# A four-layer graph network on one core: one layer's bias moves into centred weights, another's type bias moves from TensorE to VectorE

## The reference

```python
# layer 0: attention over the incoming edges, plus bias
x = layernorm(x + attention(x, edges) + bias)
# layer 1: W1 is 256x256, W2 is 256x128
h_neigh = segment_sum(h[src], dst) / maximum(deg, 1)
x = layernorm(h + relu((concatenate([h, h_neigh]) @ W1 + b1) @ W2 + b2))
# layer 2: one weight matrix for each of 8 edge types
x = layernorm(h + segment_sum((h @ weight[rel])[src], dst))
# layer 3: 3 edge types, 3 node types
parts = [relu(h)] + [segment_sum(where(type == t, relu(h[src] @ W_e[t].T + b_e[t]), 0), dst) for t in range(3)]
agg = concatenate(parts)                          # 512 features
updated = agg @ W_n[node_type].T + b_n[node_type]
x = layernorm(updated + h)
```

## Time and profile before

| | |
|---|---|
| median of 3 runs | 1756.77 us (1755.32 to 1764.27) |
| the profiled execution's own time, its span | 1757.07 us, 1755.0 us |
| PE busy, share of the span | 1439.8 us, 82% |
| PEld | 920.1 us, 52% |
| DVE | 1389.7 us, 79% |
| ACT | 1078.8 us, 61% |
| POOL | 1230.9 us, 70% |
| mean granted TensorE clock | 0.926 |

### The profile page before, as it was taken

How to read it: one execution, slowest core, us unless ns; L and a number is a source line. 1 busy time by engine, 2 the same in 40 slices (tenths; PEclk the granted TensorE clock), 3 DMA queues, 4 the chain that set the end, 5 groups by cost and what they waited for, 6 DMA issues and landing times.

```text
span 1755.0 us, 22874 instructions
## 1 busy us (share of the span) xinstructions
PE 1439.8 (82%) x6228; PEld 920.1 (52%) x6228; DVE 1389.7 (79%) x2964; ACT 1078.8 (61%) x2688; POOL 1230.9 (70%) x910
## 2 busy tenths in 40 slices
PE   2678777877887738888878589999996799999995
PEld 1445544554554526666666445565563455555553
DVE  3889999999999937989788579999997466666663
ACT  0467777777777755999889836666665233333331
POOL 7477666667766737888885188888882678888864
PEclk8799999999999968999888899999999899999998
DMA  5343444444444334777665445555542433333320
GB/s 149 73 93 99 111 107 101 103 106 105 101 110 110 76 105 121 200 193 200 173 192 150 141 105 144 135 151 142 133 122 77 102 90 91 92 95 94 91 72 22
DMA packets 165794, 205.06 MB, mean 117 GB/s; under 512 B 66824, under 2 KB 97919, under 8 KB 165667
## 3 DMA queue, kind: packets, MB, share of 16 engines
q1 hardware_dynamic: 108066, 179.45, 38.3%
q0 software_dynamic: 57600, 24.15, 7.9%
HBM read 147.12 MB, written 70.80 MB: 124 GB/s over the span
## 4 chain that ended last, share of the span: by engine, by line
PE 45%; DVE 24%; issue 11%; ACT 11%; POOL 4%; DMA 3%; SPq 1%; POOLq 0%; DVEq 0%; ACTq 0%
PE po L1211 22%; PE pt L1196 4%; DVE masked L867 4%; PE po L1206 4%; DVE bst L663 4%; PE pb L1434 4%; ACT res L952 3%; DVE run L738 2%; PE po L1269 2%; ACT x L952 2%; POOL slot_all L475 2%; DVE po L707 2%; DVE po L706 1%; DVE y L698 1%; DVE y L703 1%
## 5 line engine op out<-in xcount | busy, mean ns | idle before, releaser
L475 POOL DMA_INDIRECT xs<-target_rows,slot_all x276 | 387.6, 1404 | 192.9 <-DMA xs<-source_rows 112.1
L952 ACT ACTIVATE x<-y,nmr,rst 125x128 f32<-125x128 f32 x800 | 322.6, 482 | 41.6 <-DVE nmr L688 40.2
L1211 PE MATMUL po<-wnt,rt 128*125 128x384 f32 x800 | 305.0, 529 | 0.5 <-ACT rt L989 0.5
L475 POOL DMA_INDIRECT xs<-in_x,src_all x100 | 142.3, 1423 | 121.9 <-issue 121.9
L1211 PEld LDWEIGHTS po<-wnt,rt 128*125 128x125 f32 x800 | 168.2, 210 | 112.5 <-issue 33.4
L1211 PE MATMUL po<-wnt,run 128*125 128x384 f32 x600 | 201.5, 486 | 0.0
L1206 PE MATMUL po<-ball,ones_bf 128*125 128x512 bf16 (+1 forms) x512 | 147.6, 416 | 63.9 <-DVE sel L709 56.1
L1196 PE MATMUL pt<-ident,x 125*128 125x125 f32 x800 | 127.5, 284 | 77.8 <-issue 54.6
L482 POOL DMA_INDIRECT out_rows<-do,last_all x100 | 140.0, 1400 | 72.1 <-issue 52.3
L952 ACT ACTIVATE do<-yd,nmr,rst 125x128 f32<-125x128 f32 x400 | 163.7, 482 | 5.8 <-DVE nmr L688 5.8
L952 ACT ACTIVATE res<-sel,nmr,rst 125x128 f32<-125x128 f32 x400 | 163.6, 482 | 1.7 <-DVE nmr L688 1.7
(11 more groups left out here) (185 smaller groups left out, 3009.8 us busy)
## 6 DMA issues: line engine op xcount, KB each, us to landing
xin<-in_x SPq DMA_DIRECT2D x100, 224.0 KB
out_rows<-res SPq DMA_DIRECT2D x100, 224.0 KB
same<-same_d SPq DMA_DIRECT2D x75, 250.0 KB
source_rows<-so SPq DMA_DIRECT2D x75, 224.0 KB
target_rows<-do SPq DMA_DIRECT2D x75, 224.0 KB
xs<-source_rows SPq DMA_DIRECT2D x69, 224.0 KB
xd<-target_rows SPq DMA_DIRECT2D x59, 224.0 KB
rel<-in_etype SPq DMA_DIRECT2D x50, 250.0 KB
```

What stands on the lines that cost most here:

```text
L475: return nc.gpsimd.indirect_dma_start(out=to, out_offset=None, in_=table, in_offset=bass.IndirectOffsetOnAxis(ap=index, axis=0), bounds_ch ...
L952: last = A(to[:, j, :], y[:, j, :], ACT.Identity, scale=rst[s][:, k:k + 1], bias=nmr[s][:, k:k + 1])
L1211: last = mm(po[0:R, j * 512:j * 512 + NT * D], left(j), wnt[:, k, :, :].rearrange("k t d -> k (t d)"), start=False, stop=stop, skip_group_ ...
```

## The change

**Layer 1's bias.** Setup subtracts from W1 (`w1t`) the mean over the 128 input features, for each half. Layernormed rows sum to zero over the features, so the product is the same; and a column of the weights that sums to zero can take the bias, spread as 1/128 on each entry, if 1.0 is added to each turned feature. So `wab[:, 0]` gets b/128 added, ScalarE adds 1.0 where it evacuates the turned `x1` (`xt`) and layer 1's turned edge rows (`st`, `dt`), and the bias products of `pa`, `pb` and the fourth slot go. `bedge` goes, and `brow`, `brest`, `bhi`, `bmid`, `blo` and `ball` have three rows of bias, not four.

**Layer 3's type bias.** In layer 3 the bias products go altogether. ScalarE copies type 0's bias to `brows` (the buffers y0_0 and y0_1, free by then), VectorE overwrites it by type and adds twice the target row into `yd`, all in `doubled_rows(c)` at the end of the pass before; `updated_rows` keeps the two copies in `po` and adds its slot to `yd`. New semaphores are "bs" (type rows copied) and "xb" (doubled rows done). The dense blocks keep the bias products for their type slots, 384 columns wide.

```diff
+        brows = y0[0:2]
...
+            parts = w1t[:, :, :].rearrange("p k (a d) -> p (k a) d", a=2)
+            step(V.tensor_reduce(w1sum[:, :], parts, AX_X, ALU.add))
+            V.scalar_tensor_tensor(out=parts, in0=w1sum[:, :].unsqueeze(2).broadcast_to([D, 4, D]), scalar=-1.0 / D, in1=parts,
+                                   op0=ALU.mult, op1=ALU.add)
             V.tensor_copy(b1m[:, :, :], b1c[:, :].unsqueeze(2).broadcast_to([D, 2, D]))
-            V.memset(ball[:, :, :], 0.0)
-            step(V.memset(bedge[:, :, :], 0.0))
+            step(V.memset(ball[:, :, :], 0.0))
...
-            V.tensor_copy(wab[:, :, :], po[:, 0:2 * D].rearrange("k (a d) -> k a d", a=2))
+            V.tensor_copy(wab[:, 1, :], po[:, D:2 * D])
             V.tensor_tensor(wr[:, 1:REL, :], wr[:, 1:REL, :], wr[:, 0:1, :].broadcast_to([D, REL - 1, D]), ALU.subtract)
-            step(V.tensor_tensor(brow[:, NT, :], bank[0][:, 0:D], b2row[:, :], ALU.add))
+            step(V.tensor_tensor(b2row[:, :], bank[0][:, 0:D], b2row[:, :], ALU.add))
+            V.scalar_tensor_tensor(out=wab[:, 0, :], in0=b2row[:, :], scalar=1.0 / D, in1=po[:, 0:D], op0=ALU.mult, op1=ALU.add)
...
+            def doubled_rows(c):
+                b, q = c % 2, ph[3]
+                dve.wait_ge(q["bs"], c + 1)
+                step(V.copy_predicated(brows[b][:, :, :], bc(ntd_all[:, c, :]), type_rows(1)))
+                step(V.copy_predicated(brows[b][:, :, :], bc(ntd2_all[:, c, :]), type_rows(2)))
+                dve.wait_ge(q["xd"][c % 3], counted(c, ROWS, 3))
+                dve.wait_ge(q["nD"], at(c - 1))
+                V.scalar_tensor_tensor(out=yd[b][:, :, :], in0=xd3[c % 3][:, :, :], scalar=2.0, in1=brows[b][:, :, :],
+                                       op0=ALU.mult, op1=ALU.add).then_inc(q["xb"], 1)
             def updated_rows(c):
                 b, q = c % 2, ph[3]
                 dve.wait_ge(q["pR"], c + 1)
+                dve.wait_ge(q["xb"], c + 1)
                 step(V.copy_predicated(of_type(0), bc(ntd_all[:, c, :]), of_type(1)))
                 step(V.copy_predicated(of_type(0), bc(ntd2_all[:, c, :]), of_type(2)))
-                dve.wait_ge(q["nD"], at(c - 1))
-                V.scalar_tensor_tensor(out=yd[b][:, :, :], in0=xd3[c % 3][:, :, :], scalar=2.0, in1=of_type(0),
-                                       op0=ALU.mult, op1=ALU.add).then_inc(q["rd"], 1)
+                V.tensor_tensor(yd[b][:, :, :], yd[b][:, :, :], of_type(0), ALU.add).then_inc(q["rd"], 1)
...
                     message_sums(c + 1)
                 if c >= 1:
                     scales((c - 1) % 2, 1, ph[3]["vN"])
+                if there(c):
+                    doubled_rows(c)
...
-                    A(xt[:, :, :], by_tile(pt), ACT.Copy).then_inc(s_xt, 1)
+                    A(xt[:, :, :], by_tile(pt), ACT.Copy, bias=1.0).then_inc(s_xt, 1)
...
+            def type_rows3(c):
+                q = ph[3]
+                act.wait_ge(q["xb"], at(c - 1))
+                A(brows[c % 2][:, :, :], type_rows(0), ACT.Copy).then_inc(q["bs"], 1)
...
                     results3(c - 1)
+                if there(c + 1):
+                    type_rows3(c + 1)
...
-            def biased(to):
-                mm(to[0:R, 0:T * D], ones_bf[:, 0:R], bedge[:, :, :].rearrange("k j d -> k (j d)"), start=True, stop=False, skip_group_check=True)
-            def biased_slots(n):
+            def biased_slots():
                 for j in range(T):
-                    mm(po[0:R, j * 512:j * 512 + n * D], ones_bf[:, 0:R], ball[:, 0:n, :].rearrange("k s d -> k (s d)"), start=True, stop=False, skip_group_check=True)
-            def types(left, k, stop=True):
+                    mm(po[0:R, j * 512:j * 512 + NT * D], ones_bf[:, 0:R], ball[:, :, :].rearrange("k s d -> k (s d)"), start=True, stop=False, skip_group_check=True)
+            def types(left, k, start=False, stop=True):
                 for j in range(T):
-                    last = mm(po[0:R, j * 512:j * 512 + NT * D], left(j), wnt[:, k, :, :].rearrange("k t d -> k (t d)"), start=False, stop=stop, skip_group_check=True)
+                    last = mm(po[0:R, j * 512:j * 512 + NT * D], left(j), wnt[:, k, :, :].rearrange("k t d -> k (t d)"), start=start, stop=stop, skip_group_check=True)
                 return last
-            def product(to, left, right, stop=True):
+            def product(to, left, right, start, stop):
                 for j in range(T):
-                    last = mm(to[0:R, j * D:(j + 1) * D], left(j), right, start=False, stop=stop and j == T - 1, skip_group_check=True)
+                    last = mm(to[0:R, j * D:(j + 1) * D], left(j), right, start=start and j == 0, stop=stop and j == T - 1, skip_group_check=True)
                 return last
...
-                biased(pa)
-                product(pa, lambda j: tile_of(st, j), wab[:, 0, :])
+                product(pa, lambda j: tile_of(st, j), wab[:, 0, :], start=True, stop=True)
             def target_products1(c):
                 q = ph[1]
                 pe.wait_ge(q["rd"], c)
                 pe.wait_ge(q["eD"], c + 1)
-                biased(pb)
-                product(pb, lambda j: tile_of(dt, j), wab[:, 0, :], stop=False)
+                product(pb, lambda j: tile_of(dt, j), wab[:, 0, :], start=True, stop=False)
...
                 own, sums = (dt, agg)[c % 2], (run, run2)[c % 2]
-                biased_slots(NT)
-                types(lambda j: tile_of(own, j), 0, stop=False)
+                types(lambda j: tile_of(own, j), 0, start=True, stop=False)
```

More of the change, by code:

```diff
@@ L96, in gnn_kernel @@
         bias_bc = sb("bias_bc", [R, D])
-        brow = sb("brow", [D, NT + 1, D])
+        brow = sb("brow", [D, NT, D])
         b2row = sb("b2row", [D, D])
-        brest = sb("brest", [D, NT + 1, D])
-        bhi, bmid, blo = (sb(n, [D, NT + 1, D], BF16) for n in ("bhi", "bmid", "blo"))
-        ball, bedge = sb("ball", [D, NT + 1, D], BF16), sb("bedge", [D, T, D], BF16)
+        brest = sb("brest", [D, NT, D])
+        w1sum = sb("w1sum", [D, 4])
+        bhi, bmid, blo = (sb(n, [D, NT, D], BF16) for n in ("bhi", "bmid", "blo"))
+        ball = sb("ball", [D, NT, D], BF16)
         ones_f = sb("ones_f", [D, 1])
@@ L638, in _ @@
             for part, p in ((bhi, 0), (bmid, 32), (blo, 64)):
-                V.tensor_copy(ball[p:p + 1, :, :], part[p:p + 1, :, :])
-                last = V.tensor_copy(bedge[p:p + 1, :, :], part[p:p + 1, NT:NT + 1, :].broadcast_to([1, T, D]))
+                last = V.tensor_copy(ball[p:p + 1, :, :], part[p:p + 1, :, :])
             last.then_inc(s_bp, 1)
@@ L1009, in only_dense, with evacuate_sources, evacuate_targets @@
                 results_of(d, k % 2, 1)
-            def evacuate_sources(c, p, k):
+            def evacuate_sources(c, p, k, plus=0.0):
                 q = ph[p]
                 act.wait_ge(q["tS"], c + 1)
-                A(st[:, :], bank[k][:, 0:C], ACT.Copy).then_inc(q["eS"], 1)
-            def evacuate_targets(c, p, k, to, func):
+                A(st[:, :], bank[k][:, 0:C], ACT.Copy, bias=plus).then_inc(q["eS"], 1)
+            def evacuate_targets(c, p, k, to, func, plus=0.0):
                 q = ph[p]
                 act.wait_ge(q["tD"], c + 1)
-                A(to[:, :], bank[k][:, 0:C], func).then_inc(q["eD"], 1)
+                A(to[:, :], bank[k][:, 0:C], func, bias=plus).then_inc(q["eD"], 1)
             def slopes0(c):
@@ L1091, in _ @@
                 results_of(d, k % 2, 2)
-            evacuate_sources(0, 1, 7)
-            evacuate_targets(0, 1, 7, dt, ACT.Copy)
+            evacuate_sources(0, 1, 7, 1.0)
+            evacuate_targets(0, 1, 7, dt, ACT.Copy, 1.0)
             evacuate_rt(block_of(1, 0) - 2)
-            evacuate_sources(1, 1, 7)
+            evacuate_sources(1, 1, 7, 1.0)
             evacuate_xt(block_of(1, 0) - 2)
-            evacuate_targets(1, 1, 7, dt, ACT.Copy)
+            evacuate_targets(1, 1, 7, dt, ACT.Copy, 1.0)
             first_roots(chain_of(block_of(1, 0)) % 2, 6)
@@ L1175, in _ @@
             evacuate_sources(1, 3, 0)
+            act.wait_ge(s_x1, NC)
+            act.wait_ge(s_ln, chain_of(NC - 1) + 1)
+            type_rows3(0)
             for c in range(EC + 1):
@@ L1404, in _ @@
                 pe.wait_ge(q["vA"], c + 1)
-                product(pb, lambda j: tile_of(agg, j), wab[:, 1, :]).then_inc(q["pR"], 1)
+                product(pb, lambda j: tile_of(agg, j), wab[:, 1, :], start=False, stop=True).then_inc(q["pR"], 1)
                 d = block_of(1, c)
```

11 lines of the change are left out of this document (6 added, 5 removed).

## The result

The changed kernel takes 1742.2 us (median of four runs, 1736.5 to 1744.3) against 1756.9 for the kernel before on the same chip: a ratio of 0.989, with a 95% interval of 0.986 to 0.992. Two later comparisons, with runs of the kernel before beside them, gave 0.988 (0.984 to 0.991) and 0.989 (0.987 to 0.991). By the ratios some 19 to 22 us are gained, by the medians of the three comparisons 15, 21 and 18; I forecast 21.7. The time lies 7 us above the 1735 of the prediction and inside its range.

A forecast was written before the change was run, and what follows sets the result against it. Four bounds: TensorE in layer 3, nearly VectorE in layer 0, ScalarE and GpSimd in layer 1, VectorE in layer 2. Gains 15.0 + 3.2 + 1.5 + 2 + 0 = 21.7 us gave 1735 us, range 1728 to 1745.

The forecast's parts named there:

- Layer 3, 15.0 us: Layer 3: bias products leave TensorE's chain, 16.2 us over 25 chunks, less 1.2 us of bubbles, giving 15.0 us.
- the bubble of 0.05: Layer 3: TensorE's type products would start 0.05 us late after VectorE's release, in 24 chunks, 1.2 us.
- The cover on VectorE: Layer 3: the new VectorE operations and ScalarE copy fit into waiting and cost nothing; without cover 67 us.
- the room of 4.7 us: Layer 3: VectorE's gap per chunk of 5.3 us, less 0.6 us of chunk shrinkage, left for the new operations.
- its lead: Layer 3: GpSimd's gathers come 7.7 us early, more than a lag of 6.4 us over 20 chunks.
- The rival (12 in 100): Layer 3: new operations hold GpSimd issues, its round becomes 14.42 us, 5.7 us are lost, 1741 us; 12 in 100.
- Layer 0, 3.2 us: Layer 0: the burst behind sel shortens by 0.22 us, so VectorE's wait before y falls in 15 chunks, 3.2 us.
- the rival with 1728: Layer 0: more bursts at full clock remove both VectorE waits, 6 to 10 us more, 1728 us; 10 in 100.
- Layer 1, 1.5 us: Layer 1: TensorE mostly waits, so only first and last chunks gain from dropped bias products; 1.5 us, bounds 0 and 4.
- Layer 2's end and the blocks, 2 us: Dense blocks around layers 1 and 2 and layer 2's last three chunks have TensorE in the chain; 2 us.
- Setup, 0: Setup: VectorE work added and removed about cancels; taken as 0, bounds a loss and a gain of 1 us.
- The slower rival (3 in 100): Layer 3: two GpSimd issues held for a whole new operation in every chunk, 26 us lost, 1761 us; 3 in 100.

The follow-up runs named there:

- more3: The changed kernel with three more idle repeats of a VectorE copy by type in layer 3; 1741.0 us, ratio 0.989 to the kernel before.
- exposed: The changed kernel with layer 3's three new VectorE operations issued behind the wait for TensorE's last product; 1820.5 us, ratio 1.035 to the kernel before.
- l1_only: The kernel before with only the part of layer 1's bias, layer 3 keeping its bias products; 1756.3 us, ratio 0.998.
- a3: The changed kernel once more, unchanged, with more rounds, for a further profile; 1740.8 us, ratio 0.989 to the kernel before.
- b3: The kernel before once more, unchanged, for a further profile; 1761.5 us, one run.
- b4: The kernel before once more, unchanged, for another further profile; 1765.5 us, one run.
- c_before: The kernel before once more, unchanged, for a second trace; its layer 0 took 543.3, middle 775.9 and layer 3 365.6 us.

## Why the prediction was right, and where it was off

**Layer 3, 15.0 us: right.** 365.8 against 350.9 in the means. The price of 0.65 us, the bubble of 0.05 and the length of 13.75 came out to the hundredth. The signs named were a chunk of 13.70 to 13.80, VectorE at 10.9 and TensorE at 1.00, and all are there.

**The cover on VectorE: right, and tested.** Three operations of 2.15 us (taken as 2.1) and a copy on ScalarE of 0.62 (taken as 0.6) cost nothing. `more3` shows the room of 4.7 us: 2.15 and another 2.28 fit. What the cover is worth was mis-sized. I gave 2.7 us x 25 = 67 us for all of it, ScalarE's copy included, and left the clock out; `exposed` pays 79 us for VectorE's 2.15 alone, since the clock falls as well.

**GpSimd: the rival happened, for one round.** I had its own round at 14.07 us, 0.32 over the new chunk, and counted on its lead and on another phase. The rival (12 in 100) added a hold by a new operation and had 14.42 us, in 20 rounds. The first full round of layer 3 in the changed kernel, VectorE and GpSimd:

```profile
1413.76 3.56 DVE L744 TENSOR_TENSOR_SCAN run<-same,run,masked 128x500 f32<-128x500 f32 x3
1414.03 1.98 POOL L485 DMA_INDIRECT out_rows<-do,last_all  x1 [0.30 <-issue]
1416.31 2.10 POOL L478 DMA_INDIRECT xs<-target_rows,slot_all  x1 [0.30 <-issue]
...
1418.64 0.73 DVE L927 COPY_PREDICATED y<-ntd_all,brow 125x512 f32<-125x512 int32 x1
1418.72 1.78 POOL L478 DMA_INDIRECT xs<-target_rows,slot_all  x1 [0.30 <-issue]
...
1423.95 1.23 POOL L485 DMA_INDIRECT out_rows<-do,last_all  x1 [0.30 <-issue]
```

The two old holds are there as in the earlier trace rows, a third issue of 1.78 us beside the new operations, and the round, from the scatter at 1409.46 to that at 1423.95, takes 14.49: the rival, to 0.07 us, of which part is luck, since the third issue is held for 0.51 us (1.78 against 1.27) where the rival had 0.35, and another issue is 0.09 shorter than before. It moves GpSimd's phase by 0.74 us against the chunk, and from the next round on the scatters start every 13.75 us (1437.70, 1451.46, 1465.20). In the new phase the long issues are 1.64, 1.95 and 1.43 us, so each is shorter. What is wrong in the rival is that it multiplied one round by 20, and what is right in the forecast is that holds depend on the phase. The Trainium skill ("SBUF — State Buffer", Who interferes with whom) says that VectorE instructions with two SBUF inputs contend with a GpSimd instruction that reads SBUF. The trace agrees, for old and new operations, and shows how long an issue is held: the one of 1460.31 ends at 1461.74, 1.13 us after the second new copy (1460.61), the one of 1454.50 at 1456.14, 1.05 us after the masking (1455.09). It is a copy by type that holds the issue; no issue starts during the doubling (1460.64 to 1461.33), which the prediction had named. My sign, a gap of 0.30 before the first scatter, is there (0.31), and no round of TensorE waits for gathered rows.

**Layer 0, 3.2 us: right, a little small.** It gave 4.1 in the means (545.1 and 541.0) and 4.2 in `l1_only`. The step from 1.09 to 0.86 us in the burst is the 0.22, and the wait before y fell from 0.54 to 0.32. I counted the 15 chunks for which the view of waits shows that wait; with 13 to 15 steady rounds that go from 23.68 to 23.47 the mechanism gives 2.7 to 3.2 us. The rest lies in rounds of other lengths (22.5 to 25 us), whose number differs from profile to profile, and it is not explained. Over all 14 profiles, those of the experiments included, layer 0 takes 545.5 us in the mean without this part of the change and 541.8 with it, 3.7 us less. The wait before tmp stayed at 0.42 in most chunks, and no steady chunk got the microsecond of the rival with 1728.

**Layer 1, 1.5 us: not seen.** TensorE has 14 us less to do there (265.15 for 279.37) and waits at least that much more. Its waits in the changed kernel, the answer to the earlier trace rows, with the one for gathered rows beside it:

```profile
PE pt L1225 <- issue: 48.8, 17, 14.0
PE pc L1225 <- DMA xs<-target_rows,slot_all: 45.9, 10, 21.6
```

In the same window the four profiles before have 34.7 to 49.9 us in the first of these waits and 29.8 to 39.2 in the second, together 67.8 to 85.7; the three after have 92.3 to 94.7 together. The 25 aggregations of layer 1 take 298.3 to 301.4 us before and 298.2 to 301.5 after: the work that is gone has become waiting.

**Layer 2's end and the blocks, 2 us: the step that failed.** "The dense blocks that run alone before layers 1 and 2 and after layer 2 [...] have TensorE in the chain". Between layers 1 and 2 they do, and they are shorter; but what follows there waits for something else. The chain of the kernel after between layers 1 and 2:

```profile
988.58 1.28 PE po L1231 x4
...
997.30 0.86 PE po L1231 x4
998.16 2.58 PE po L1236 x8
...
1001.61 7.04 issue
1008.66 1.08 PE pc L1225 x4
```

The two bursts of bias rows took 1.71 and 1.08 us before, so 0.65 us are saved here as forecast. The wait behind the last block is 7.04 us (6.76 in `a3`), where the kernel before has 4.88 (5.73 in `b3`). The view names only the issue as what ends it; the timeline shows that TensorE then turns layer 2's first gathered rows, and that GpSimd asks for them only when its wait for source rows has ended:

```profile
1000.53 1.27 POOL L478 DMA_INDIRECT xs<-target_rows,slot_all  x1 [54.82 <-DMA xs<-source_rows]
...
1008.66 1.07 PE L1225 MATMUL pc<-ident,xs 125*128 125x125 f32 x4 [7.04 <-issue]
```

From that issue to the turn it is 7.5 and 8.2 us before (first profile and `b3`) and 8.1 and 8.0 after (first profile and `a3`), whenever the block ended. So a block that ends sooner meets a longer wait. After layer 2 the bias rows of the last block turn out not to be in the chain. It runs from ScalarE's rt to the type products, first in the kernel before and then in the changed one:

```profile
1347.12 2.85 PE L1211 MATMUL po<-wnt,rt 128*125 128x384 f32 x8 [0.51 <-ACT rt L989]
```

```profile
1346.54 4.54 PE L1236 MATMUL po<-wnt,rt 128*125 128x384 f32 x8 [0.77 <-ACT rt L1007]
```

The bias rows ahead of them take 0.86 us for 1.08, and the wait for rt is 0.26 longer. The forecast also left out the clock: the granted clock of these products is 1.00 in the first profile before and 0.62 in the one after, 1.69 us more. That is not the change's doing, since `b3` and `b4`, the kernel before again, have 4.54 us there as well and `c_before` has 2.85; it is one part of the spread of the middle that the trace names. That the whole of the forecast's 2 us went into longer waits was not tried by an experiment; the middle only shows no gain, and with its spread of 6 us it could hide one of this size.

**Setup, 0: right.** Layer 0's first copy comes at 50.4 us before and 50.0 after, in profiles that differ by 1.6 among themselves.

**The sum.** Means over the profiles are 15.0 + 4.1 + 0.4 - 2.8 = 16.7 us; the three comparisons give 19 to 22 with an interval of some 5 on each side. Of the 3.5 us for layers 1 and 2 nothing can be seen, and layer 0 gave 0.9 more. The rest of the distance between 1735 and 1742 is within the spread of the executions (the medians of the changed kernel are 1742.2, 1739.4 and 1740.8), and the profile of before, from which I subtracted, had the shortest middle of its four.

**The slower rival (3 in 100)** did not come: in the steady rounds only one issue is held by a new operation, and for a short time. `exposed` does not price that rival, since it puts the operations themselves into TensorE's path. What it prices is the change without cover: 1820 us, where my 67 us would give 1802.

## What to carry to other kernels

Take work off the engine that a stage's chain runs through, and put it where the timeline shows another engine waiting for that same engine: 0.65 us of TensorE per chunk were worth 0.60, and 2.15 us of VectorE were worth nothing while 5.3 us of waiting stood there. In a stage where the engine waits for gathered rows (layer 1, the start of layer 2) the same saving only makes the next wait longer, so follow a saved microsecond to the release that comes last before it is put into the sum. And take the profile of before more than once: a term of 2 us can't be read off one execution whose middle varies by 6.

## What the runs showed of the hardware that was not expected

- With a wait of 2.08 us of TensorE in every round the clock was down for the burst behind it in 13 of 22 rounds, at 1.69 us each. With a wait of 1.38 us in every round it was down in none, behind the one wait of 2.33 us in the changed kernel it stayed at 1.00, and behind the last chunk's waits of 3.89 and 4.58 us it was down, at 3.04 and 2.2 us. The same block of one and the same kernel can get either clock: 2.85 or 4.54 us for the eight products after layer 2. In the rounds that lost clock the exposed operations cost 3.96 us for 2.27 of their own.
- GpSimd's round in layer 3 locked to the chunk, with every gap at 0.30 or 0.31 us from its second round on. Its issues were held according to where they start in VectorE's operations; one round of 14.49 us moved the phase by 0.74, the long issues of 1.98, 2.10 and 1.78 us became 1.64, 1.95 and 1.43, and from then on nothing slipped. A sum of holds at one phase says nothing of the next.
- A copy by type with all operands in SBUF takes 0.73 us where the one in `po` takes 0.70, over 125x512; ScalarE's copy of that size takes 0.62.
